# A decoder layer on one core: bias of the self-attention output in the sum, inverse sums in strips, gate logits and last scores in another order

## What is computed

```
x = x + cross_attention(layernorm(x), ctx, bias, mask)   # 16 heads of 32, 2048 keys, padded
x = x + self_attention(layernorm(x))
x = x + experts(layernorm(x))
```

```
probs = clamp(softmax(clamp(q @ k.T)));  o = clamp(probs @ v)
return clamp(o @ Wo.T + bo)
```

## Time and profile before

| | us |
|---|---|
| median of 3 runs | 452.39 (452.37 to 452.97) |
| the profiled execution, its own time | 454.42 |
| span of the profiled execution, first to last instruction | 452.7 |
| PE busy in the span | 440.6 (97%) |
| DVE busy | 367.3 (81%) |
| ACT busy | 302.2 (67%) |
| POOL busy | 87.0 (19%) |
| mean granted TensorE clock | 0.990 |

### The profile page before, as it was taken

The page is one execution under the profiler, slowest core; times in us unless marked ns, Lnnn a source line. Parts: engine busy times, 40 slices in busy tenths (PEclk is TensorE's granted clock), DMA queues, the critical chain, the costliest instruction groups (busy, mean ns, idle before and its releaser), DMA issues.

```text
span 452.7 us, 9864 instructions
## 1 busy us (share of the span) xinstructions
PE 440.6 (97%) x3428; PEld 365.8 (81%) x3428; DVE 367.3 (81%) x516; ACT 302.2 (67%) x622; POOL 87.0 (19%) x111
## 2 busy tenths in 40 slices
PE   8999999999998999999999999999999999999995
PEld 3888888888887789878888787878788787878795
DVE  6889777777779876668978989888989898998972
ACT  4637666666666643667274878787777878777852
POOL 7100000000000122000133250505041230505002
PEclk9999999999999999999979999999999999999999
DMA  7980000000000921800000499999999999998002
GB/s 263 381 295 26 25 23 23 23 23 23 23 26 21 340 89 66 262 19 3 1 0 1 168 387 386 385 387 387 385 332 350 351 307 349 312 376 304 28 1 93
DMA packets 43105, 82.02 MB, mean 181 GB/s; under 512 B 2632, under 2 KB 3784, under 8 KB 43080
## 3 DMA queue, kind: packets, MB, share of 16 engines
q1 hardware_dynamic: 41816, 81.09, 51.0%
q10 hardware_dynamic: 1264, 0.59, 0.5%
HBM read 80.57 MB, written 1.10 MB: 180 GB/s over the span
## 4 chain that ended last, share of the span: by engine, by line
PE 89%; DVE 6%; DMA 1%; issue 1%; ACT 1%; DVEq 0%; POOL 0%; SPq 0%
PE po L1699 19%; PE pk L1699 11%; PE pv L1699 10%; PE pk L1306 8%; PE pv L1316 6%; PE ps L1335 5%; PE ps L1415 3%; PE pv L1335 3%; PE po L1725 3%; PE ps L1460 3%; PE po L1428 2%; PE ps L1408 2%; PE po L1335 2%; DMA x_s<-in_x 1%; PE pk L1335 1%
## 5 line engine op out<-in xcount | busy, mean ns | idle before, releaser
L1242 DVE TENSOR_TENSOR w_lo<-att_w,w_hi 128x2048 fp32r<-128x2048 f32 x60 | 138.0, 2309 | 21.3 <-ACT w_hi L705 21.3
L705 ACT CAST w_hi<-att_w 128x2048 fp32r<-128x2048 f32 x60 | 115.1, 1918 | 15.5 <-PE po L1699 15.5
L488 ACT ACTIVATE big_a<-ps,negm 128x128 f32<-128x128 f32 x176 | 62.2, 394 | 0.0
L1699 PE MATMUL po<-w_hi,ht_hi 128*128 128x512 f32 (+1 forms) x128 | 50.0, 391 | 0.0
L1699 PE MATMUL po<-w_hi,ht_lo 128*128 128x512 f32 (+1 forms) x128 | 48.6, 380 | 0.0
L1699 PE MATMUL po<-w_lo,ht_hi 128*128 128x512 f32 (+1 forms) x128 | 48.6, 380 | 0.0
L1306 PE MATMUL pk<-ctx_s,att_w 128*128 128x128 f32 x352 | 42.1, 278 | 0.0
L1306 PEld LDWEIGHTS pk<-ctx_s,att_w 128*128 128x128 f32 x352 | 40.2, 192 | 1.9 <-issue 1.8
L488 ACT ACTIVATION_READ_ACCUMULATOR big_a<-ps,negm 128x1 f32 x176 | 41.1, 233 | 0.0
L908 DVE TENSOR_REDUCE mc<-ps 128x8 f32<-128x1024 f32 x22 | 26.9, 1221 | 10.0 <-PE ps L1408 9.9
L1699 PEld LDWEIGHTS po<-w_hi,ht_lo 128*128 128x128 f32 x128 | 24.0, 188 | 5.0
(11 more groups left out here) (348 smaller groups left out, 1027.0 us busy)
## 6 DMA issues: line engine op xcount, KB each, us to landing
att_w<-in_w SPq DMA_DIRECT2D x64, 1024.0 KB, 7.2
ctx_s<-in_ctx_t SPq DMA_DIRECT2D x11, 256.0 KB, 2.7
x_s<-in_x SPq DMA_DIRECT2D x4, 256.0 KB, 4.0
att_w<-in_wk SPq DMA_DIRECT2D x1, 1024.0 KB, 8.0
att_w<-in_wq SPq DMA_DIRECT2D x1, 1024.0 KB, 10.4
att_w<-in_wv SPq DMA_DIRECT2D x1, 1024.0 KB, 11.9
att_w<-in_sv SPq DMA_DIRECT2D x1, 1024.0 KB, 14.6
att_w<-in_wo SPq DMA_DIRECT2D x1, 1024.0 KB, 14.8
```

The costliest lines, as they stand in the source:

```text
L488: ins = a.activation(big_a[:, h], ps[:, c, g * P:(g + 1) * P], ACT.Exp, bias=negm[:, h:h + 1], accum_out=sums[:, h:h + 1])
L705: a.copy(w_hi[:, i % SLOTS], att_w[:, i]).then_inc(hi_ok, 1)
L1242: v.tensor_tensor(w_lo[:, i % SLOTS], att_w[:, i], w_hi[:, i % SLOTS], ALU.subtract).then_inc(lo_ok, 1)
L1699: ins = mm(dst, l, r, start=start and i == 0, stop=i == len(terms) - 1, skip_group_check=True)
```

## The change

Six things are changed, all of them with the same result in exact arithmetic.

1. *Bias in the sum.* POOL makes three bf16 rows whose sum is the bias bo, in partitions 0, 32 and 64 of a tile of zeros (`so_rows`), by 8 instructions after its other constants. The tiles lie in the memory of `state`, which is no longer read by then. Each product of `out_project` begins with one more matmul, of ones with these rows. DVE's addition of `bo_b` goes: the clamp reads the bank.
2. *Inverse sums in strips, for batches 2 and 3.* `values2` gives the sums in another order of heads, so that `spread_inverse` is four matmuls with 32 rows each, on four different groups of rows of the array, into the four banks `ps`. It waits for all exponentials (`e2_ok`) and for the bank's reader of the batch before (`pv2_out`). POOL makes the 32-row matrices (`strip_spread`) by 4 small copies.
3. *Logits of batch 0* are made between `out_project(2)` and `out_project(3)` and no longer after `turn_gate(2)`; they wait for `normalise(3)`. The transposed x of batch 0 is put in bank 7, and `out_project(3)` waits until it has been copied out.
4. *Top-k and slots from PSUM.* The copies L1192 and L1209 go; `max`, `match_replace` and the comparison read the bank.
5. *Fillers* before the transpose of the probabilities: 3 and no longer 5.
6. *Last scores.* In the last pass of the chunk loop `scores` and the transpose of batch 0 come before the last quarter of the value projection.

```
+                for i in range(KC):      # POOL, then 8 instructions for so_rows
+                    g.tensor_copy(strip_spread[r].rearrange("p (c d) -> p c d", d=DH),
+                                  ident[r, i * DH:i * DH + KC].unsqueeze(2).broadcast_to([DH, KC, DH])).then_inc(spread_ok, 1)
...
             def self_bias(b):
                 dve.wait_ge(o2_mm, b + 1)
-                link(v.tensor_tensor(norm[:, b], banks[OUT_BANKS[b]], bo_b[:], ALU.add))
-                v.tensor_scalar(norm[:, b], norm[:, b], LO, HI, ALU.max, ALU.min).then_inc(o2_out, 1)
+                v.tensor_scalar(norm[:, b], banks[OUT_BANKS[b]], LO, HI, ALU.max, ALU.min).then_inc(o2_out, 1)
...
-            link(v.tensor_copy(prob_t, pv[0:B * E, 0:T]))
-            src = prob_t
+            src = pv[0:B * E, 0:T]
...
-            link(v.tensor_copy(slot_t[:], pk[:, 0:B * E]))
...
-                v_project(t + 1, 3)
-                scores(t + 1)
                 if at_end:
+                    scores(t + 1)
                     turn_batch(1, 0)
+                    v_project(t + 1, 3)
+                else:
+                    v_project(t + 1, 3)
+                    scores(t + 1)
                 values(t)
...
             def spread_inverse(b):
                 pe.wait_ge(inv_ok, b + 1)
+                if b >= 2:
+                    pe.wait_ge(e2_ok, 2 * B)
+                    pe.wait_ge(pv2_out, b)
+                    for g in range(KC):
+                        r = slice(g * DH, (g + 1) * DH)
+                        ins = mm(ps[:, g, 0:T], strip_spread[r], row_sums[r], start=True, stop=True, skip_group_check=True)
+                    ins.then_inc(inv_mm, 1)
+                    return
...
-                project(1, b, banks[OUT_BANKS[b]], o2_mm)
+                now = slice(b * T, (b + 1) * T)
+                product(banks[OUT_BANKS[b]], [(ones3[:], so_rows[:])] + [(t[:, k, now], w[:, 1, k]) for k in range(KC)
+                                                                     for w, t in ((w_hi, tr_hi), (w_lo, tr_hi), (w_hi, tr_lo))]).then_inc(o2_mm, 1)
...
             turn_gate(0)
             out_project(2)
+            gate_project(0)
             out_project(3)
             turn_gate(1)
             turn_gate(2)
-            gate_project(0)
...
-            keep_busy(5, 4)
+            keep_busy(3, 4)
```

More of the change, by code:

```diff
@@ L66, in decoder_layer @@
         tr_gate = qt
-        state = sb("state", [P, B, D])
+        running_sums = ExitStack()
+        state = running_sums.enter_context(nc.sbuf_tensor("state", [P, B, D], F32))
+        running_sums.close()
+        so_rows = sb("so_rows", [P, D], BF16)
+        so_part = sb("so_part", [P, D], BF16)
+        so_rest = sb("so_rest", [P, D])
+        sb("rest_of_state", [P, 2 * D])
         total = sb("total", [P, B, H])
@@ L153, in decoder_layer @@
         spread = q_now
+        strip_spread = ctx_s[:, 2]
         of_group = ctx_s[:, 3].rearrange("p (g m) -> p g m", g=KC)
@@ L1088, in normalise @@
                 dve.wait_ge(ot2_out, b + 1)
-                v.tensor_tensor(norm[:, b], norm[:, b], sums2(b), ALU.mult).then_inc(pv2_out, 1)
+                if b < 2:
+                    v.tensor_tensor(norm[:, b], norm[:, b], sums2(b), ALU.mult).then_inc(pv2_out, 1)
+                else:
+                    rows = norm[:, b].rearrange("p (g t) -> p g t", g=KC)
+                    v.tensor_tensor(rows, rows, ps[:, :, 0:T], ALU.mult).then_inc(pv2_out, 1)
                 dve.wait_ge(pv2_out, b + 1)
@@ L1109, in last_output @@
                 dve.wait_ge(last_mm, half + 1)
[L1110 to L1113, removed]
+                v.tensor_scalar(norm[:, B - 1, now], banks[LAST_OUT_BANKS[half]][:, now], LO, HI, ALU.max, ALU.min).then_inc(last_out, 1)
+                dve.wait_ge(last_out, half + 1)
                 v.tensor_tensor(x_s[:, B - 1, now], x_s[:, B - 1, now], norm[:, B - 1, now], ALU.add).then_inc(last_resid, 1)
@@ L1208, in _ @@
             dve.wait_ge(slot_mm, 1)
-            link(v.tensor_copy(slot_t[:], pk[:, 0:B * E]))
             for half in range(2):
                 now, rows = slice(2 * half, 2 * half + 2), slice(half * 2 * E, (half + 1) * 2 * E)
-                v.tensor_tensor(onehot[:, now].rearrange("p b e s -> p (b e) s"), slot_t[:, rows].unsqueeze(2).broadcast_to([P, 2 * E, CAP]),
+                v.tensor_tensor(onehot[:, now].rearrange("p b e s -> p (b e) s"), pk[:, rows].unsqueeze(2).broadcast_to([P, 2 * E, CAP]),
                                 iota_s[:].unsqueeze(1).broadcast_to([P, 2 * E, CAP]), ALU.is_equal).then_inc(onehot_ok, 1)
@@ L1559, in values2 @@
                     for c in range(STRIPS):
-                        ins = mm(sums2(b)[c * DH:(c + 1) * DH, 0:P], of_group[:, g], half[:, c * KC + g],
+                        h = c * KC + g if b < 2 else g * KC + c
+                        ins = mm(sums2(b)[c * DH:(c + 1) * DH, 0:P], of_group[:, g], half[:, h],
                                  start=g == 0, stop=g == KC - 1, skip_group_check=True)
@@ L1585, in out_project @@
                             pe.wait_ge(ot2_out, B)
-                        product(banks[LAST_OUT_BANKS[half]][:, cols_h], [(t[:, k, now], w[:, 1, k, cols_h]) for k in range(KC)
+                        product(banks[LAST_OUT_BANKS[half]][:, cols_h], [(ones3[:], so_rows[:, cols_h])] + [(t[:, k, now], w[:, 1, k, cols_h]) for k in range(KC)
                                                                  for w, t in ((w_hi, tr_hi), (w_lo, tr_hi), (w_hi, tr_lo))]).then_inc(last_mm, 1)
                     return
-                project(1, b, banks[OUT_BANKS[b]], o2_mm)
+                now = slice(b * T, (b + 1) * T)
+                product(banks[OUT_BANKS[b]], [(ones3[:], so_rows[:])] + [(t[:, k, now], w[:, 1, k]) for k in range(KC)
+                                                                     for w, t in ((w_hi, tr_hi), (w_lo, tr_hi), (w_hi, tr_lo))]).then_inc(o2_mm, 1)
             def turn_gate(b):
@@ L1622, in gate_project @@
                 pe.wait_ge(tr_hi_ok[4], b + 1)
+                if b == 0:
+                    pe.wait_ge(pv2_out, B)
                 if b == B - 1:
@@ L1679, in _ @@
                     pe.wait_ge(norm_hi_ok, B)
+                if c == 2:
+                    pe.wait_ge(onehot_ok, 2)
                 for b in (2 * pair, 2 * pair + 1):
```

29 lines of the change are left out of this document (24 added, 5 removed).

## The result

| | before | after |
|---|---|---|
| median of 8 runs each, same chip, us | 453.06 (452.37 to 454.45) | 454.58 (454.06 to 455.80) |
| ratio after to before | | 1.0034 [1.0021, 1.0047] |
| the profiled execution, its own time, us | 454.42 | 454.06 |
| its span, us | 452.7 | 452.3 |
| its mean granted clock | 0.990 | 0.993 |

The changed kernel is 1.5 us slower, where 0.5 us less had been forecast; 454.58 lies outside the range. The two profiled executions say the opposite, by 0.4 us. So the first thing to learn is that one of them is not typical: the trace of the kernel before is of an execution 1.4 us above that kernel's median, the trace after is of the fastest execution of the eight.

The account below looks back on a forecast made before the run. PE was taken as the chain at the gate, with fillers at half clock holding up the slots' transpose. Fillers ending 0.3 us earlier plus the copy's 0.22 gave 0.52, so 452.39 - 0.5 = 451.9 us; range 450.5 to 453.1.

Parts of the forecast that it names:

- Every sign that the prediction named: Profile after: low clock from 232 to near 239, exponential at 233.6, comparison at 240.7; clock 1.00 throughout or 0.50 beyond 240 refutes.
- The second copy: DVE's copy of the transposed slots before the comparison, 240.95 to 241.17: on the chain, its removal gains 0.22 us.
- Fillers 5 to 3: Before the transpose of the probabilities: fillers end before these are ready, so their number costs no time, only affects the clock.
- rival B: Gate: with fewer fillers the clock comes back later, deciding at 239.9; slower by 0.55 to 1.05 us; 14%.
- Exponential 0.6 us earlier: ACT's exponential at the gate moves from 234.22 to 233.6, right behind ACT's normalise; bounds 0.1 and 0.75 us.
- fillers' block 0.8 us: Before the gather: the transpose of the slots, ready at 239.90, stood in PE's queue behind fillers for 0.8 us.
- Logits of batch 0: Gate logits, moved ahead of out_project(3): cost PE 0.79 us wherever they stand; logits finished at 232.4 in place of 233.26.
- DVE's statistics: After out_project(3): L1124 moves from 231.99 to some 231.8, a gain of 0.2 us.
- Bias in the sum: out_project: DVE saves 0.47 us for each of three batches; PE pays 0.25 per added matmul, in all 1.0 us.
- Strips: Spreads of inverse sums, batches 2 and 3: 0.29 us in place of 0.89, 0.6 saved each; mode changes might cost 0.5.
- Top-k and slots from PSUM: First copy, 0.31 us, gains nothing where fillers end later; reading PSUM costs up to 0.1 us; second copy gains 0.22.
- Last scores and POOL: Last scores put earlier: 0 us, bounds -0.1 and +0.4; POOL's twelve more instructions fit its idle time: 0 us.

Follow-up runs that it names:

- b_shift: Kernel before with only slot_t's 128 bytes per partition taken out, so later tiles lie where the changed kernel has them; 454.68 us, ratio 1.0025.
- a_again: The changed kernel, unchanged, timed once more against the kernel before on another chip; 455.02 us, ratio 1.0036.
- a_pad: The changed kernel with slot_t's 128 bytes per partition kept as an unused tile, 3 fillers; 454.11 us, ratio 1.0006.
- b_fill3: The kernel before with only the fillers ahead of the transpose of the probabilities cut from 5 to 3; 453.89 us, ratio 1.0005.
- b_again: The kernel before, unchanged, timed and profiled once more; 453.22 us, ratio 0.9993.
- a_pad_fill5: The changed kernel with slot_t's bytes kept as an unused tile and 5 fillers in place of 3; 452.76 us, ratio 0.9994 to the kernel before.
- b_line: The kernel before with 32 unused bytes per partition ahead of iota_s, so tr_hi begins at 177,792; 449.44 us, ratio 0.9917.
- a_scores_back: The changed kernel with the last scores again behind the last quarter of the value projection; 454.91 us, ratio 1.0028 to the kernel before.
- a_line_hold: The changed kernel with 5 fillers, tr_hi at 177,792, and 4 more fillers around the gate's last transposes; 450.05 us, ratio 0.9918 to the kernel before.

## Why the prediction was wrong

Measured: +1.5 us, in place of -0.5. The two us between them come from the steps below. (Of the distance from 451.9 to 454.58 another 0.7 us is the starting point: the kernel before had a median of 452.39 in 3 runs and of 453.06 in 8.)

Every sign that the prediction named lay ahead of 242 us. Those that were to refute it hardly show in the trace after: the clock was not at 1.00 all through nor at 0.50 beyond 240, the exponential came at 233.33, and only `out_project(3)` ends later than before, by 0.04 us (228.02). Some of the others missed: the low clock was to begin at 232, and the comparison, at 239.86, was to come at 240.7. But the loss is in the experts, for which no sign was named.

**The step that was missing: a removed tile moves its neighbours.** "The second copy, 240.95 to 241.17, is on the chain: 0.22 us" was all that the prediction said of removing `slot_t`. That the tile's 128 bytes go, and that every operand declared behind it moves, was in no step and no rival. It cost 1.1 us in the kernel before (b_shift, 1.0025; 1.4 by the medians) and 0.9 to 1.4 us in the changed one (a_again less a_pad, by medians and by ratios): most of the loss. In the traces 0.96 us of it are the experts: 0.82 for seven and 0.14 for the last. The prediction left them out as untouched; they are 44% of the span, and a per cent of their pace is 2 us.

**Fillers 5 to 3.** "Their number costs nothing in time; their part is in the clock" is right as a sentence and was then given no price, only rival B at 14%. Its condition was met in one trace with 3 fillers, not in the trace after: the clock was back at 240.3 in b_fill3, later than the deciding point of 239.9. And a low mean clock came in most executions with 3 fillers (46 of 74), not in one of seven. But it came in a quarter of those with 5 too, so what the fillers cost is the difference of two shares, about 0.4 us, and not 0.55 to 1.05.

**Exponential 0.6 us earlier, fillers' block 0.8 us.** Both were differences to one execution with the long stretch of low clock. Counted from the first scores of the self-attention (at 195.86, 196.25, 195.34 and 195.36), in us:

| | before | b_again | after | a_pad_fill5 |
|---|---|---|---|---|
| low clock at the gate | 6.8 | 3.4 | 3.4 | 3.4 |
| last matmul of the logits | 37.03 | 36.61 | 36.77 | 36.74 |
| exponential | 38.36 | 37.92 | 37.99 | 37.96 |
| slots ready | 44.03 | 43.55 | 43.61 | 43.61 |
| gather | 46.06 | 45.04 | 45.27 | 44.87 |

At the shorter low stretch, b_again against after, no edit ahead of the slots gained anything, and the block of the transpose was not there to be relieved. The lead of 1.31 us is thus 0.52 us from ahead of the self-attention, of which 0.47 is older than any edit (a product at the start of the kernel begins at 10.93 in the trace after and at 11.40 in the trace before, and at 11.00 in b_line, which has the code of before), and 0.79 us in this stretch, where the same program differs by 1.02 us between its own two traces.

**Logits of batch 0.** "Cost PE 0.79 us wherever they stand" is the step that failed here. They went where the prediction had them, 0.79 us at 224.14. But in the kernel before they stood where PE would otherwise wait for ACT's copies of the transposes. The chain of the kernel before:

```profile
227.98 0.87 PE ps L1605 x8
...
231.84 1.41 PE po L1628 x8
```

From the transposes of batches 1 and 2 to the last eight logit matmuls it was 231.84 - 227.98 = 3.86 us, and it is 231.47 - 228.02 = 3.45 after. So of the 0.79 us only 0.41 came back; for the rest PE now waits (the copy L658 in the chain above). The last logits are ready 0.16 us later than in b_again, by the table. The forecast had PE done with them at 232.4 and it was, by luck: the start was 0.52 us early, and the last eight matmuls took 0.91 us and not 1.41, as the clock had not fallen yet.

DVE's statistics gained the forecast 0.2 us: from the first scores to L1124 (L1152 after) it is 36.12 in b_again and 35.92 after. ACT's normalise, at 232.34 + 0.82 = 233.16, follows them. But the exponential at 233.33 waits for DVE's `gsm`, that is for the logits (the row of ACT above), and not for ACT's normalise as forecast. What one path gained the other lost.

**Bias in the sum.** DVE's clamp from the bank takes 0.68, as forecast. On PE 13 matmuls take 3.12 us, where 12 took 3.00 in the chain of b_again: 0.12 for one bf16 matmul and not 0.25. The two of 256 columns in the last batch cost 3.08 - 2.81 = 0.27 together. In all about 0.6 us and not 1.0: mis-sized, in the change's favour.

**Strips.** A spread takes 0.43, not 0.29; it was 0.89. Saved 0.46 each and not 0.6: mis-sized by 0.3 us in all, against the change. The Trainium skill's page "TensorEngine Tiling (Array Packing)", Key Properties, has a drain at a change of mode. The 0.14 us above the estimate of 0.29 have its sign, and are less than the quarter of a us that I had put on it. No run here parts the drain from the four matmuls.

**Top-k and slots from PSUM.** `max` from the bank takes 0.29, from SBUF 0.28, so reading the bank costs nothing to speak of. The first copy was forecast to gain nothing where fillers end later. It gains nothing for another reason. Behind the rounds stands one operation on DVE (L1203, L1230 after), and beside it three subtractions on POOL. b_again, then the kernel after:

```profile
238.69 0.36 DVE L1203 TENSOR_SCALAR kt_s<-ctx_s 32x128 f32<-32x128 f32 x1
235.19 3.77 POOL L376 TENSOR_TENSOR tr_lo<-norm,tr_hi 128x512 fp32r<-128x512 f32 x3 [1.77 <-DVE gsm L1189]
...
237.46 0.74 DVE L1230 TENSOR_SCALAR kt_s<-ctx_s 32x128 f32<-32x128 f32 x1
234.37 3.75 POOL L381 TENSOR_TENSOR tr_lo<-norm,tr_hi 128x512 fp32r<-128x512 f32 x3 [2.06 <-DVE gsm L1217]
```

The same operation takes 0.22 us in the trace before and 0.74 after, and in all 18 traces of this study it ends 0.07 to 0.12 us behind POOL's third subtraction. Both start from the same number, the last of the softmax, and the slots are ready 4.66 to 4.71 us behind that in every trace, with the copy and without. So the 0.31 us of the first copy were spent waiting. That POOL holds DVE back there is read from these times; no run moved POOL's work away. The second copy is gone from the chain. In the trace after the fillers stand where it was; where they do not (a_pad_fill5) the gather is 0.17 us earlier than in b_again, by the table, about the 0.22 forecast for this copy less the 0.06 by which the slots are late. The gather now also waits, at its third bank, until the second comparison has read the slots; the chain after has no gap there.

**Last scores and POOL.** 0, as forecast: a_scores_back differs from a_again by 0.0008 with intervals of 0.0012 to either side; POOL's new instructions are done at 182.3, and the first matmul that reads them is at 211.45.

**All edits together**, with the tile's bytes kept and 5 fillers, come to -0.3 us (a_pad_fill5, 0.9994 [0.9980, 1.0008]). At 177,792 the changed kernel with 5 fillers has 0.9916 and 0.9928 in its two runs, the kernel before (b_line) 0.9917. No measurable gain, against -0.5 forecast. With 0.9 to 1.4 for the address and 0.4 for the fillers this sums to 1.0 to 1.5 us; measured was 1.5. The terms are from different chips, and each ratio has an interval of some 0.6 us to either side, so that they add up says little.

A version that beats both kernels is neither's edit: 32 unused bytes in the kernel before, 449.44 us. The changed kernel at these addresses with five fillers is not faster: 449.54 and 450.17.

Open: why a start at a multiple of 128 bytes is faster for 512 columns and slower for 256, and which tile it is. It is not the operand of 512 columns in the experts: `w_hi` and `w_lo` are declared ahead of `slot_t` and never moved. What moved are the tiles that PE loads as weights there (`ht_hi`, `ht_lo`, `xin_hi`, `xin_lo`) and those that ACT, DVE and POOL read and write beside it; all moved together, and no run parts them. Open too is what decides where in an execution the clock falls.

## What to carry over

A change that removes or resizes a tile is two changes: keep the bytes, and time the edit, then try the address by itself; here 128 bytes cost about a us, and six edits together gained nothing that could be measured. Before a forecast of some tenths of a per cent is built on a wait in one trace, compare that trace's own time with the median: 2 us between them were a sign here that the wait need not be typical. And read the untouched stages as well after a change: equal instructions with another mean duration say at once that it is no question of order.

## What the runs showed of the hardware

- The pace of fp32r products depends on where their tiles lie in SBUF. 36 products of 512 columns took 8.42, 8.39, 8.19 to 8.22 and 8.40 us with `tr_hi` at 177,632, 177,760, 177,792 and 177,856, and the 36 products of 256 columns took 4.28, 4.21, 4.32 and 4.11. In all it moved this kernel by 1.1%, from b_shift (ratio 1.0025) to b_line (0.9917), 4.9 us.
- The granted clock of one program fell at another place in each execution, between 231.1 and 234.8, and was low for 3.4 or for 6.8 us in every trace looked at, never in between. The executions with the lower mean clock take 1.0 to 1.3 us longer, in the kernel before.
- It fell with PE busy in the whole stretch (1.00 in a_line_hold) as well as with PE idle for 1.19 us shortly before (the kernel after).
- Top-k's `max` on 32x128 took 0.29 us from PSUM and 0.28 from SBUF.
- A DVE operation from SBUF to SBUF on 32x128 took 0.22 to 0.74 us beside subtractions of 128x512 on POOL, and ended 0.07 to 0.12 us behind the third of these in all 18 traces.
